# Attention with weighted sums in pairs of blocks, a sum spread by a matmul, and biased scores in SBUF

## The reference

```
q, k, v = heads of x @ Wq.T + bq, x @ Wk.T + bk, x @ Wv.T + bv
gate    = sigmoid(a) * (sigmoid(b) * gru_const - 1) + 2      # a, b: per token and head
scores  = q k^T / 4 + gate * pos_bias                        # pos_bias: by relative position and head
out     = softmax(scores over keys) @ v                      # 8 x 16 x 1024 x 1024 scores
```

## Time and profile before

| | us |
|---|---|
| median of 3 runs | 4017.55 (4009.93 to 4023.25) |
| profiled execution | 4000.15 |
| its span | 3998.3 |
| TensorE busy | 3523.8 (88%), weight loads 2750.0 |
| VectorE busy | 2410.7 (60%) |
| ScalarE busy | 2381.2 (60%) |
| GpSimd busy | 1221.6 (31%) |
[...]

### The profile page before, as it was taken

The page is one execution under the profiler, slowest core; times in us unless marked ns, Lnnn a source line. Parts: engine busy times, 40 slices in busy tenths (PEclk is TensorE's granted clock), DMA queues, the critical chain, the costliest instruction groups (busy, mean ns, idle before and its releaser), DMA issues. The chain is left out here.

```text
span 3998.3 us, 97133 instructions
## 1 busy us (share of the span) xinstructions
PE 3523.8 (88%) x33340; PEld 2750.0 (69%) x33716; DVE 2410.7 (60%) x5410; ACT 2381.2 (60%) x4590; POOL 1221.6 (31%) x1533
## 2 busy tenths in 40 slices
PE   4994998998989989989999899785699999999993
PEld 2552776776767767767677677675588888888882
DVE  3664998898889988989889899576011111111115
ACT  2553998898989989989889899311222222222221
POOL 1332332332323323323233233037322222222221
PEclk9996999999999999999999999896799999999996
DMA  5667242242432332424232423564455555555556
GB/s 172 203 206 151 31 83 55 39 88 43 95 63 37 71 66 31 96 41 93 55 49 68 70 31 73 143 206 143 172 172 190 173 187 177 184 190 172 193 178 204
DMA packets 243211, 468.95 MB, mean 117 GB/s; under 512 B 35474, under 2 KB 138772, under 8 KB 224146
## 3 DMA queue, kind: packets, MB, share of 16 engines
q1 hardware_dynamic: 200466, 393.04, 37.1%
q0 software_dynamic: 26880, 35.87, 4.2%
q10 hardware_dynamic: 15360, 33.56, 2.4%
HBM read 309.87 MB, written 152.58 MB: 116 GB/s over the span
## 5 line engine op out<-in xcount | busy, mean ns | idle before, releaser
L660 DVE CUSTOM_DVE_ANT_0 sc<-sc,gbias 128x1024 f32<-128x1024 f32 x1024 | 1261.7, 1233 | 274.6 <-issue 198.9
L713 ACT ACTIVATE probs<-sc,negm 128x1024 f32<-128x1024 f32 x1024 | 1141.3, 1115 | 190.4 <-DVE negm L660 188.1
L569 POOL TENSOR_SCALAR gbias<-slab_a,gs 128x484 f32<-128x484 f32 x1024 | 683.8, 668 | 1487.6 <-DVE negm L660 1456.5
L602 PEld LDWEIGHTS pt<-ident,probs 128*128 128x128 f32 x8192 | 966.5, 142 | 203.2 <-issue 11.4
L602 PE MATMUL pt<-ident,probs 128*128 128x128 f32 x8192 | 1070.5, 274 | 1.4 <-issue 1.1
L724 ACT ACTIVATE pts<-pt 128x512 f32<-128x512 f32 x1280 | 733.6, 595 | 10.8 <-PE pt L602 10.6
L1211 ACT ACTIVATE f_hid<-f_ph,f_w_up 128x256 f32<-128x256 f32 x576 | 272.6, 473 | 719.0 <-PE f_ph L1172 719.0
L584 PE MATMUL sc<-ks,qs 128*128 128x512 bf16 x1672 | 542.2, 389 | 164.8 <-issue 68.7
L620 PE MATMUL pop<-pts,vs 128*32 128x128 f32 x16384 | 603.3, 277 | 18.0 <-DVE pts L670 6.3
L670 DVE COPY pts<-pt 128x512 f32<-128x512 f32 x768 | 525.5, 684 | 8.8 <-PE pt L602 8.8
L1172 PE MATMUL f_ph<-f_xt,f_w_up 128*128 128x256 f32 x2304 | 511.5, 380 | 2.6 <-DMA f_w_up<-in_w_up 1.9
(11 more groups left out here) (155 smaller groups left out, 2274.8 us busy)
## 6 DMA issues: line engine op xcount, KB each, us to landing
f_w_down<-in_w_down SPq DMA_DIRECT2D x72, 1152.0 KB, 5.3
f_w_up<-in_w_up SPq DMA_DIRECT2D x72, 1028.0 KB, 7.7
xg_d<-fill SPq DMA_DIRECT2D x16, 1820.0 KB, 16.5
ks<-k_d SPq DMA_DIRECT2D x192, 128.0 KB
qs<-q_d SPq DMA_DIRECT2D x192, 128.0 KB
f_xin<-xg_d SPq DMA_DIRECT2D x72, 260.0 KB, 5.2
v_d<-vt SPq DMA_DIRECT2D x16, 1024.0 KB, 6.5
vs<-v_d SPq DMA_DIRECT2D x32, 512.0 KB
```

What stands on the lines that cost most here:

```text
L569: pool.tensor_scalar(gbias[r % 4][:, SIDE:SIDE + BAND], slab[:, r % 4, :], gs[k % 2][:, r // 4, r % 4:r % 4 + 1], 1.0, ALU.mult, ALU.mult) ...
L602: mm = pe.transpose(pt[:, bank(k, r, half), j, :], probs[:, r % 2, jj * P:(jj + 1) * P], ident[:])
L660: dve.tensor_tensor_reduce(sc[:, r % 2, :], sc[:, r % 2, :], gbias[r % 4][:, w:w + N], -1.0, 3.0e38, ALU.add, ALU.min, negm[:, r % 4:r % 4 ...
L713: act.activation(probs[:, r % 2, :], sc[:, r % 2, :], ACT.Exp, bias=negm[:, r % 4:r % 4 + 1], scale=-1.0, accum_out=sums[:, i % 2, hh:hh + ...
```

## The change

- `weigh` works on pairs of blocks (8 rows): `pts` holds 256 query columns for each j and head, a matmul has 256 moving columns. There are four parts of two j, in TensorE's places x % 8 = 0 to 3 of the next pair.
- The exponential has no accumulator output. The row sums are taken from the ones column of `vs`, which gives row 16 of each head's 32 partitions in `po`. ScalarE copies `po` (128x256) to `raw` at x % 8 = 4; TensorE multiplies `raw` by the constant `sum_row`, which spreads each head's sum over its 32 partitions into `pr`, at x % 8 = 5; VectorE takes the reciprocal of all of `pr` (128x256) to `inv` and multiplies `raw` by it, at x % 8 = 6, between bias-and-max x and the copy of row x - 2. `reciprocals` and `copy_sums` are gone.
- `bias_and_max` writes to `tot`, three buffers in SBUF, from which the exponential reads. The scores of row x + 2 wait for the maximum of row x, no longer for its exponential; bias-and-max x waits for exponential x - 3.

```diff
     bias_and_max(k, r):
+    dve.wait_ge(exp_done, m * R + (r - 2 if k > 0 or r > 2 else 0))
-    dve.tensor_tensor_reduce(sc[:, r % 2, :], sc[:, r % 2, :], gbias[r % 4][:, w:w + N], -1.0, 3.0e38,
+    dve.tensor_tensor_reduce(tot[:, (k * R + r) % 3, :], sc[:, r % 2, :], gbias[r % 4][:, w:w + N], -1.0, 3.0e38,
...
-    act.activation(probs[:, r % 2, :], sc[:, r % 2, :], ACT.Exp, bias=negm[:, r % 4:r % 4 + 1], scale=-1.0,
-                   accum_out=sums[:, i % 2, hh:hh + 1]).then_inc(exp_done, 1)
+    act.activation(probs[:, r % 2, :], tot[:, (k * R + r) % 3, :], ACT.Exp, bias=negm[:, r % 4:r % 4 + 1], scale=-1.0).then_inc(exp_done, 1)
...
-    for j in range(3 * part, min(3 * part + 3, NI)):
+    for j in (2 * part, 2 * part + 1):
         for hh in range(4):
-            mm = pe.matmul(po[32 * hh:32 * hh + 32], vs[k % 2][:, j, 32 * hh:32 * hh + 32], pts[:, i % 2, hh, j, :],
+            mm = pe.matmul(po[32 * hh:32 * hh + 32], vs[k % 2][:, j, 32 * hh:32 * hh + 32], pts[:, i // 2 % 2, hh, j, :],
...
+def spread_sums(k, i):
+    pe.wait_ge(raw_done, m * NP2 + i // 2 + 1)
+    pe.matmul(pr, sum_row[:], raw[:], start=True, stop=True).then_inc(sums_done, 1)
...
     # TensorE's loop
-    for x in range(len(rows) + 4):
+    for x in range(len(rows) + 6):
         if x < len(rows):
+            if x + 2 < len(rows):
+                pe.wait_ge(max_done, (body * STEPS + rows[x][0]) * R + rows[x][1] + 1)
+                scores(*rows[x + 2])
             pe.wait_ge(exp_done, (body * STEPS + rows[x][0]) * R + rows[x][1] + 1)
-            if x + 2 < len(rows):
-                scores(*rows[x + 2])
             turn(*rows[x])
-        if x >= 4:
-            k, r = rows[x - 4]
-            if r % 4 < 3:
-                weigh(k, r // 4, r % 4)
+        if x >= 8:
+            k, r = rows[(x - 8) // 8 * 8]
+            if x % 8 < 4:
+                weigh(k, r // 4, x % 8)
+            elif x % 8 == 5:
+                spread_sums(k, r // 4)
...
     def finish(k, i):
+        dve.wait_ge(sums_done, m * NP2 + i // 2 + 1)
+        dve.reciprocal(inv[:], pr).then_inc(inv_done, 1)
...
-        dve.tensor_tensor(ot[:, k % 2, i * P:(i + 1) * P], po, rsb[:], ALU.mult).then_inc(ot_done[k % 2], 1)
+        dve.wait_ge(inv_done, m * NP2 + i // 2 + 1)
+        dve.tensor_tensor(ot[:, k % 2, i * P:(i + 2) * P], raw[:], inv[:], ALU.mult).then_inc(ot_done[k % 2], 1)
...
     # VectorE's loop
         if x < len(rows):
             bias_and_max(*rows[x])
-        if x >= 6 and rows[x - 6][1] % 4 == 3:
-            finish(rows[x - 6][0], rows[x - 6][1] // 4)
+        if x >= 14 and x % 8 == 6:
+            finish(rows[(x - 14) // 8 * 8][0], rows[(x - 14) // 8 * 8][1] // 4)
         if 2 <= x <= len(rows) + 1:
-            k, r = rows[x - 2]
-            copy_out(k, r)
-            if r % 4 == 3:
-                reciprocals(k, r // 4)
+            copy_out(*rows[x - 2])
...
+    def copy_raw(k, i):      # ScalarE, after exponential x, ahead of the copies of row x - 1
+        act.wait_ge(av_done, m * NP2 + i // 2 + 1)
...
+        act.activation(raw[:], po, ACT.Copy).then_inc(raw_done, 1)
...
+        if x >= 12 and x % 8 == 4:
+            copy_raw(rows[(x - 12) // 8 * 8][0], rows[(x - 12) // 8 * 8][1] // 4)
```

More of the change, by code:

```diff
@@ L86, in shape_constants @@
     c["c_ident"] = np.eye(P, dtype=np.float32)
+    c["c_sums"] = (np.arange(P)[:, None] == np.arange(P)[None, :] // 32 * 32 + D).astype(np.float32)
     c["c_order"] = np.broadcast_to(np.arange(NE, dtype=np.float32) - NE, (P, NE))
@@ L467, in attend @@
         probs = sb("probs", [P, 2, N])
-        pts = sb("pts", [P, 2, 4, NI, P])
+        pts = sb("pts", [P, 2, 4, NI, 2 * P])
         negm = sb("negm", [P, 4])
[L470 to L473, removed]
+        sum_row = sb("sum_row", [P, P])
+        raw = sb("raw", [P, 2 * P])
+        inv = sb("inv", [P, 2 * P])
         ot = sb("ot", [P, 2, N])
+        tot = sb("tot", [P, 3, N])
         sc = es.enter_context(nc.psum_tensor("sc", [P, 2, N], F32))
@@ L535, in _ @@
                             sp.dma_start(slab[:], slab_d[:, bass.ds(g * 4, 4), :]).then_inc(slab_in, 16)
[L537 removed]
+                        sp.wait_ge(ot_done[kk], uses(body, k) * NP2)
                         for s in range(6):
@@ L667, in copy_out @@
                             dve.wait_ge(tr_done, (m * R + r + 1) * 2)
[L668 to L678, removed]
+                            if hh == 1 and i % 2 == 0:
+                                dve.wait_ge(av_done, pairs_before(m, k, i))
@@ L685, in finish @@
-                        dve.wait_ge(av_done, m * NI + i + 1)
-                        dve.tensor_tensor(ot[:, k % 2, i * P:(i + 1) * P], po, rsb[:], ALU.mult).then_inc(ot_done[k % 2], 1)
-                    for x in range(len(rows) + 6):
+                        dve.wait_ge(inv_done, m * NP2 + i // 2 + 1)
+                        dve.sem_inc(sums_seen, 1)
+                        dve.tensor_tensor(ot[:, k % 2, i * P:(i + 2) * P], raw[:], inv[:], ALU.mult).then_inc(ot_done[k % 2], 1)
+                    for x in range(len(rows) + 7):
@@ L721, in copy_out @@
                                 act.wait_ge(tr_done, (m * R + r) * 2 + half + 1)
-                                if hh == 0 and half == 0:
-                                    act.wait_ge(av_done, blocks_before(m, k, i))
-                                act.activation(pts[:, i % 2, hh, 4 * half:4 * half + 4, :], pt[:, bank(k, r, half)], ACT.Copy).then_inc(copied_a, 1)
-                    def copy_sums(k, i):
+                                if hh == 0 and half == 0 and i % 2 == 0:
+                                    act.wait_ge(av_done, pairs_before(m, k, i))
+                                act.activation(pts[:, i // 2 % 2, hh, 4 * half:4 * half + 4, i % 2 * P:(i % 2 + 1) * P], pt[:, bank(k, r, half)], ACT.Copy).then_inc(copied_a, 1)
+                    def copy_raw(k, i):
                         m = body * STEPS + k
-                        act.wait_ge(av_done, m * NI + i + 1)
-                        act.activation(rsb[:], pr, ACT.Copy).then_inc(rcopied, 1)
+                        act.wait_ge(av_done, m * NP2 + i // 2 + 1)
+                        act.wait_ge(inv_done, m * NP2 + i // 2)
+                        act.wait_ge(ot_done[k % 2], uses(body, k) * NP2 + i // 2)
+                        act.wait_ge(ot_done[(k + 1) % 2], uses(body, k + 1) * NP2)
+                        act.activation(raw[:], po, ACT.Copy).then_inc(raw_done, 1)
                     def store(k):
-                        act.wait_ge(ot_done[k % 2], (uses(body, k) + 1) * NI)
+                        act.wait_ge(ot_done[k % 2], (uses(body, k) + 1) * NP2)
                         act.dma_start(ot_d[bass.ds(g, 1), bass.ds(bb * STEPS + k, 1)].rearrange("o w p n -> p (o w n)"), ot[:, k % 2, :]).then_inc(ot_stored[k % 2], 16)
-                    for x in range(len(rows) + 5):
-                        if x > R and x % R == 10:
+                    for x in range(len(rows) + 6):
+                        if x > R and x % R == 16:
                             store(x // R - 1)
@@ L739, in _ @@
                             exponential(*rows[x])
-                        if x >= 5 and rows[x - 5][1] % 4 == 3:
-                            copy_sums(rows[x - 5][0], rows[x - 5][1] // 4)
+                        if x >= 12 and x % 8 == 4:
+                            copy_raw(rows[(x - 12) // 8 * 8][0], rows[(x - 12) // 8 * 8][1] // 4)
                         if 1 <= x <= len(rows):
```

34 lines of the change are left out of this document (19 added, 15 removed).

## The result

The changed kernel takes 4615.53 us, the median of four runs (4599.56 to 4636.15), beside 4013.74 of the kernel before (four runs, 4009.64 to 4023.25). The ratio is 1.1498, with a 95% interval of 1.1445 to 1.1552. The forecast was 4560 with a range of 4400 to 4670. A later comparison of the same two kernels gave 4627.0 beside 4013.47 and a ratio of 1.1535 (1.1513 to 1.1557).

What follows compares the result with a forecast made beforehand. TensorE was taken as the bound, with next to no stall. The profiled 4000.15 us, 17.4 to the median and +442 of waits gave 4460; about 100 for the clock gave 4560, range 4400 to 4670.

Steps and rivals of the forecast that it cites:

- The slots: TensorE's weighing: a new part takes 1.02 us, its slot 2.41; a pair without stall 15.75 against 16.18.
- The reciprocal: VectorE's finishing: a reciprocal of 256 elements takes 1.75 us, by the slope of its own rows.
- rival two: The wait holds but the reciprocal is an ordinary pass (0.425): 1.35 less a pair, no falls, 4300 us; chance 0.07.
- The place argument: VectorE's finish at place 14 stands still 1.8 us for the sums; TensorE idles 2.1 and 0.8; a pair takes 19.8.
- The rival of the hidden wait: The wait before the reciprocal is under 0.3 us, TensorE stays the bound, a pair 15.75: 3975 us; chance 0.07.
- The sum of waits: Attention, eight bodies of 128 rows: each body 55.3 us longer, in all +442.
- The clock: TensorE's stops lower the clock: a fall costs about 1.7 us, half of 120 pairs taken, 102 us.
- The fourth rival: Falls in nearly every pair, stops a little longer: 4664 us, or 4710 with 0.4 us more a pair; chance 0.13.

Runs made afterwards that it cites:

- the copy: The changed kernel with a plain copy of the sums in place of the reciprocal, at the same place: 4408.35 us, ratio 1.0769.
- the kernel with the filled stop: The changed kernel with one set of TensorE's transposes in each pair done three times, 16 more instructions: 4559.66 us, ratio 1.1133.
- tot_alone: The kernel before with only three score buffers in SBUF and scores that wait for the bias-and-max, not the exponential: 4097.31 us, ratio 1.0005.
- pairs_alone: The changed kernel without the score buffers: bias and exponential work in PSUM, scores wait for the exponential: 4841.82 us, ratio 1.1818.

## Why the prediction was right, and where it was off

- *The slots.* With weighing 2.41 was predicted; the trace has 2.41 (1513.61 to 1516.02). Right: a part, half as many instructions, takes 1.01 from its start to the next scores (1512.60 to 1513.61), where an estimate from the earlier trace rows had 1.02, four sets at a pace of 0.216 plus 0.16 for the switch.
- *The reciprocal.* 1.75 by the slope of its rows; 1.757 measured. The ordinary pass, rival two, was wrong. The rows decide: the time does grow with each element, by (1757 - 175) / 252 = 6.3 ns. Between its first two rows, 175 at 4 and 226 at 11, the slope is 7.3, which the working's bound of 6.4 left out; by that slope the reciprocal would have been 2.0 us, so the bound held without having been earned. What rival two forecast for a short operation in that place, 1.35 less a pair and no steady falls, came out with the copy: 18.54 to 18.63 us a pair.
- *The place argument.* From TensorE's slot 12 (1499.74) on, predicted and measured: start of the reciprocal 3.9 and 3.97, idle before it 1.8 and 1.95, bias-and-max 15 at 6.05 and 6.24, scores 17 at 7.4 and 7.53, idle 2.1 and 2.12, transposes 15 at 8.8 and 8.87, idle 0.8 and 0.73. Everything is right within 0.2. The 0.4 from the end of the sum passes' issue to the reciprocal was the author's estimate, with no row behind it; from the passes' start 0.9 was predicted and 0.74 measured (1502.97 to 1503.71). The pair without falls, 19.8 against 16.18, is the 19.87 of the kernel with the filled stop. The rival of the hidden wait (3975) needed an idle time under 0.3 before the reciprocal and falls with it. It would have failed at the reciprocal's length too: with the finish one place later that idle time is 0.30, and the pair takes 18.69 and not 15.75.
- *The sum of waits.* +442 was predicted. The kernel with the filled stop has a loop 462 us longer than before (2606.2 against 2144.3). 20 us are missing. From one body's first exponential to the next's the growth is 58.2, not 55.3. Of these 3 us, 1 lies in the 14 pairs between rows 8 and 120 (278.2 against 226.5), and 2 between row 120 and the next body, where 8.4 were added and not 3.6 + 3; the rows without weighing are as forecast, 2 us less.
- *The clock.* This is the step that was mis-sized: half of the 120 pairs at 1.7, so 102. The 1.7 was an estimate, and no run shows it. In the kernel before, eight transposes took 1.91 us where the clock's share was 0.50 (1192.4 to 1196.0) and 1.04 where it was 1.00; the clock's record of every run has these two shares alone. In fact 110 of the 112 pairs have a fall, at 1.14 in the mean, and the loop loses 157 us (124 by the second trace). Count and price were both off and partly cancelled, which was luck. The forecast's 3.4 us for a fall is right for 87 of the 124; 30 last 6.8, and 7, at the bodies' ends, 10.2. The price goes by length and by place in the pair. From one reciprocal to the next a pair takes 19.94 us without a fall. With one of 3.4 us that begins at most 4.0 us after the reciprocal's start, while TensorE stands or soon behind it, it takes 20.5 (26 pairs in the first trace, 61 in the second); with one that begins later, 21.0 (61 and 36); with one of 6.8 us, 22.2 (23 and 13). So a fall of 3.4 us costs 0.6 or 1.0 and not 1.7: in the slow stretch VectorE sets the pace, with a bias-and-max every 1.75 us (1505.98, 1507.73, 1509.47), and the slower matmuls (eight transposes in 1.79 and 1.63 us, not 1.09) hide in part behind them. The count was read from stops that didn't fit: 2.0 us between dense matmuls held, but this stop comes in two pieces with two matmuls between. Shortening the first piece alone, with the second still 0.73, took the falls from 124 to 65 and 8.
- *Where it lies on the scale.* 462 + 157 + 17 outside the loop = 636, the difference of the two profiled executions. The working had 442 + 102, so 92 are missing: 20, 55 and 17. On the medians 56 are missing, since the changed kernel's profiled execution was 21 above its median and I had added 17 for the kernel before's, which lay below. The fourth rival's 0.4 us a pair on top of all falls, and so its 4710, no run shows: the reciprocal took 1.757 us, within 0.01 of the working's 1.75, and with falls in 110 of 112 pairs a pair took 21.01.

What stays open: how the 0.9 us that the score buffers give back divides between the scores' earlier issue and fewer or shorter falls, and why the falls of two executions of one kernel come at different places in the pair.

## What to carry to other kernels

A step that waited held up all that stood behind it on its engine, and those who waited for that: here 1.95 us of VectorE before the reciprocal, and 2.12 of TensorE behind it; a finishing step belongs where its input has long been there. Before an operation is made wide, its duration is to be read from rows of its own kind: a reciprocal of 256 elements took four times a copy's time (1.757 us against 0.424), and its length came through to the pair whole. When TensorE is freed of work, look at what its new gaps do to its clock (here 124 falls in the loop where there were 7, which cost 157 us, and 124 us in a second execution); and when a change has several parts, run them apart: here the paired weighing and the score buffers, with the sums done as before and the weighing in every other slot, were worth 1.3%, while the score buffers alone were worth nothing (ratio 1.0005).

## What the runs showed of the hardware

- More work on TensorE made a kernel faster: 16 redundant transposes in each stop of some 2 us took a pair from 21.01 (20.75 in a second execution) to 19.87 us, through the clock alone.
- Falls of the clock's share from 1.00 to 0.50, by the stop in each pair: 2.12 and 0.73 us, 124; 1.59 and 0.73, 65; 0.38 and 0.73, 8.
- A fall of 3.4 us lengthened a pair of 19.94 us by 0.6 or by 1.0, by where in the pair it began, and one of 6.8 us by 2.2.
- A float32 reciprocal takes 175 ns at 4 elements a partition, 226 at 11, 278 at 20 and 1757 at 256 (the changed kernel): close to a straight line, 6.3 ns an element.
- The same kernel before took 4013 us on one chip and 4093 to 4094 on two others, and the traces put the difference behind the loop (1483 to 1488 against 1559 to 1576 us); its cause wasn't looked for.
- The exponential of 1024 elements takes 1151 ns out of SBUF (the changed kernel; 1149 in `tot_alone`) and 1115 out of PSUM (the kernel before; 1118 in `pairs_alone`). The bias-and-max takes 1221 into SBUF (the changed kernel; 1225 in `tot_alone`) and 1233 in place in PSUM (the kernel before; 1231 in `pairs_alone`).
